# Attention scores from queries and keys in two fp32r parts, and y's remainder written over its source

## The chip, the cores and the metric

The kernel runs on one core of a Trainium2 chip. The metric is the device time of one execution, in microseconds (us). Five engines work side by side: TensorE (PE; its weight loads are listed as PEld), VectorE (DVE), ScalarE (ACT), GpSimd (POOL), and SyncE (SP), which here only issues transfers. Each runs its own list of instructions in order and waits for the others on semaphores.

## The reference

One layer of a vision transformer on 16 images of 256 tokens with 256 features:

```python
h = layernorm(patchify(x) @ W) * gamma
# attention, 16 heads of 64, with a decay in place of a softmax
q, k, v = silu(xn @ Wq), silu(xn @ Wk), xn @ Wv
cum = cumsum(-softplus(xn @ Wa + ba))
attn = (q @ k.T) * exp(cum[i] - cum[j])        # for j <= i
o = groupnorm(attn @ v) * gn_w + gn_b
h = h + (o * sigmoid(xn @ Wg)) @ Wo
# feed-forward: the two best of 8 experts for each token
h = h + sum(weight * (gelu(xf @ w1[e] + b1[e]) @ w2[e] + b2[e]))
```

## The kernel before, in words

The 16 images are taken in eight pairs p (`NPR`), and each pair's 16 heads in eight head pairs c (`NP`): two heads of 64 features fill the 128 partitions. An index u says which image of the pair is meant. After the attention stage comes the expert stage; it is not changed but for the place of two buffers.

All matrix products but a few small ones are of one kind: an operand is split into a high part (a copy that rounds to fp32r, made on ScalarE) and a remainder (source minus high part, made on VectorE), and `three` lists the three products high x high, high x low, low x high. The scores were an exception: plain fp32 products of queries and keys.

Every engine has its own function `step(p, c)`, in which the order of its work is written out by hand; `last_step` is step 7. Step c works on the scores of head pair c and prepares head pair c+1 (in step 7, head pair 0 of the next pair). For attention alone:

- TensorE: `scores(c, 0)`, `queries(c+1)`, `weighted(c, 0)`, `scores(c, 1)`, `keys(c+1)`, `gates(c+1)`, `weighted(c, 1)`. Between them stand parts of other work: `values`, the token projection of the next pair (`tokens`), its transposes (`turn`, L1122), `logits`, `out_proj`, routing.
- ScalarE: `keep_o` (copies the output bank, L822), `tanh_q` (L789), `decay(c+1, 0)` (four exponentials, L817), now and then `keep_v`, `affined`, `y_hi` (L835) or `softplus`, then `tanh_k` (L794), `decay(c+1, 1)`, `tanh_g`.
- VectorE: `decayed(c, 0)` (scores times decay, L1674), `silu_q(c+1)` (L1658), other work, `decayed(c, 1)`, `silu_k(c+1)` (L1665), other work. In step 2 the embedding of an image (`embed`, to L1609) stands behind `silu_k`; in step 3 its norm (`embed_norm`, L1617) does.
- GpSimd: `decay_rows` masks the decay rows of the head pair after (L654); in between it raises variances to a power (`embed_rsqrt`, L660, among others) and scatters rows.

A score call (`scores`, L1187) handles one image and one head pair. It makes for each of the two heads, in rows 0 to 63 and 64 to 127 of the array, a product of 256 columns (L1195) and one of 128 (L1198); the causal half that is not needed is left out. Queries and keys lie in two buffers each (`q_s`, `k_s`), used in turn. One tile, `tq`, takes tanh of the queries and then that of the keys.

y is the gated output of the attention. It is split too: `y_hi` writes `y_sp[0]`, `y_lo` (L1722) writes `y_sp[1]`, from `osb`, and `out_proj` multiplies both with the parts of Wo (L1237).

Of the kernel before, what the change touches and what calls it, by code (L numbers as in the profile page):

```python
# [19 lines left out]
F32 = mybir.dt.float32  # L20
# [7 lines left out]
P = 128  # L28
# [47 lines left out]
def vit_layer(nc, xT, w_tok, gamma, wq, wk, wv, wg, wa, ba, wo, gn_w, gn_b,  # L76
# [3 lines left out]
    with ExitStack() as ctx:  # L80
# [41 lines left out]

        ys = [sb(f"y_sp{j}", [P, 2048], F32R) for j in range(2)]
        y_sp = [y[:, :].rearrange("p (k n) -> p k n", k=GC) for y in ys]

        w1_sp = [parts((0, 2048), 2048, EC), parts((10240, 14336), 2048, EC)]
        w2_sp = [parts((4096, 6144), 2048, HC), [y[:, :].rearrange("p (k n) -> p k n", k=HC) for y in ys]]
# [10 lines left out]

        big_f = sb("big_f", [P, 8192])
        stage_w = [big_f[:, i:i + 2048] for i in (0, 2048, 6144)]  # L140
        tg = big_f[:, 0:4096].rearrange("p (k n) -> p k n", k=NP)
        osb = big_f[:, 4096:8192].rearrange("p (k n) -> p k n", k=NP)
        w1_f = [big_f[:, i * 2048:(i + 1) * 2048] for i in range(2)]
# [10 lines left out]
        q_s = [sb(f"q_s{i}", [P, SP2]) for i in range(2)]  # L154
        k_s = [sb(f"k_s{i}", [P, SP2]) for i in range(2)]
# [55 lines left out]
        gel_u = [x[:, i * BLK:(i + 1) * BLK] for x in q_s + k_s for i in range(2)]  # L211
# [68 lines left out]
        v_ps v_done q_ps k_ps g_ps tq_done tk_done tg_done sq_done sk_done s_ps mult_done o_ps o_done gst_done  # L280
# [66 lines left out]
        def _(sp):  # L347
# [144 lines left out]
            def load_next_early(j):  # L492
# [14 lines left out]
                if j == 1:  # L507
                    sp.wait_ge(M["sk_done"], NP * NPR)
# [237 lines left out]
        def _(act):  # L746
# [39 lines left out]
            def tanh_q(p, c):  # L786
                act.wait_ge(M["q_ps"], NP * p + c + 1)
                have(act, "sk_done", NP * p + c)
# [21 lines left out]
            def decay(p, c, u):  # L810
# [3 lines left out]
                for hh in range(2):  # L814
# [17 lines left out]
            def y_hi(p, g, j):  # L832
                act.wait_ge(M["gate_done"], 4 * p + 2 * g + j + 1)
                have(act, "wo_ps", 2 * (2 * p + g))
                act.activation(y_sp[0][:, 2 * j:2 * j + 2, :], osb[:, GC * g + 2 * j:GC * g + 2 * j + 2, :], ACT.Copy).then_inc(M["yh_done"], 1)  # L835
# [73 lines left out]
            def last_step(p):  # L909
# [17 lines left out]
                if nxt:  # L927
                    tanh_k(p + 1, 0)
                    keep_v(p + 1, 1, 0)
                    decay(p + 1, 0, 1)  # L930
                    tanh_g(p + 1, 0)

            def step(p, c):
# [167 lines left out]
        def _(pe):  # L1101
# [1120 lines left out]
```

## Time and profile before

| | us |
|---|---|
| median of 3 runs (1324.74 to 1326.38) | 1326.38 |
| the profiled execution | 1323.79 |
| its span | 1321.9 |
| TensorE busy | 1250.9 (95%) |
| ScalarE busy | 858.5 (65%) |
| VectorE busy | 825.2 (62%) |
| GpSimd busy | 428.1 (32%) |

The span goes from the first instruction of the program to the last in one profiled execution. The attention stage fills about the first 833 us of it, the expert stage the rest. Busy times are sums over an engine's instructions; TensorE's products overlap, so their single durations add up to more than the time that passes. The granted clock is the share of full speed that TensorE was given. A bracket at the end of a row of the timeline tells how long the engine was idle before it and what ended that.

### The profile page before, as it was taken

The numbers are of one execution on the slowest core, as the hardware profiler recorded it, in microseconds if no ns is written. First come the engines' busy times: TensorE is split into PE (matmuls) and PEld (weight loads), VectorE is DVE, ScalarE is ACT, GpSimd is POOL, SyncE is SP. The second block draws the span as 40 slices with busy tenths as digits, with TensorE's granted clock in tenths as the row PEclk, the third lists the DMA queues.
The fourth block names the chain that finished last, engine by engine and source line by source line (L and its number), as shares of the span: only waits on it lengthen the run. The fifth ranks groups of instructions, "written<-read, shape, count | busy, mean of one in ns | idle before, by whom it ended". The sixth has DMA issues, their size and how long they took to land. (4 is left out here: it accounts for less than half of the span.)

```text
span 1321.9 us, 27298 instructions
## 1 busy us (share of the span) xinstructions
PE 1250.9 (95%) x8534; PEld 1072.3 (81%) x8534; DVE 825.2 (62%) x2119; ACT 858.5 (65%) x2019; POOL 428.1 (32%) x524
## 2 busy tenths in 40 slices
PE   3899999999999999999999999999999999999996
PEld 2676777878778778778778778889999999989996
DVE  4455556665665665665665566657788888565552
ACT  2557577576576576576576565636788888666662
POOL 2021211241241241241141142164444544433434
PEclk7799999999999999999999999999999999999998
DMA  5321331341331331341332236458888787888873
GB/s 193 121 93 61 105 98 47 117 131 46 117 129 49 109 128 57 108 130 57 108 114 63 89 102 186 161 179 245 282 238 222 222 237 188 262 257 262 249 232 88
DMA packets 125607, 194.46 MB, mean 147 GB/s; under 512 B 16272, under 2 KB 91504, under 8 KB 125360
## 3 DMA queue, kind: packets, MB, share of 16 engines
q1 hardware_dynamic: 111920, 175.91, 41.5%
q0 software_dynamic: 13584, 17.26, 6.4%
q8 instruction: 54, 0.88, 0.3%
q14 instruction: 49, 0.40, 0.1%
HBM read 167.40 MB, written 29.05 MB: 149 GB/s over the span
## 5 line engine op out<-in xcount | busy, mean ns | idle before, releaser
L1161 PE MATMUL bank<-xn_sp,big_r 128*128 128x512 f32 x1152 | 312.1, 408 | 0.0
L1161 PEld LDWEIGHTS bank<-xn_sp,big_r 128*128 128x128 f32 x1152 | 204.6, 188 | 53.2 <-issue 1.4
L1674 DVE TENSOR_TENSOR att<-bank,dec_x 128x384 f32<-128x384 f32 x256 | 130.7, 552 | 110.1 <-PE bank L1198 108.9
L817 ACT ACTIVATE dec_x<-dec_x,ncum 128x256 f32<-128x256 f32 (+1 forms) x512 | 189.7, 444 | 5.7 <-POOL dec_x L654 5.7
L654 POOL TENSOR_SCALAR_AFFINE_SELECT dec_x<-dec_x 128x256 f32<-128x256 f32 x256 | 103.6, 434 | 215.8 <-DMA dec_x<-cum_scratch 215.7
L1494 PE MATMUL bank<-big_r 128*128 128x256 f32 x1296 | 168.0, 286 | 1.5 <-ACT mid_f L887 1.0
L1494 PEld LDWEIGHTS bank<-big_r 128*128 128x128 f32 x1296 | 160.5, 192 | 3.3 <-ACT mid_f L887 1.4
L705 POOL TENSOR_SCALAR mid_f<-mid_f,dec_x 128x256 f32<-128x256 f32 x71 | 76.9, 1087 | 187.0 <-DVE mid_f L1925 184.6
L711 POOL DMA_INDIRECT out<-mid_f,tok x71 | 118.6, 1671 | 53.0 <-POOL mid_f L705 22.0
L1941 DVE TENSOR_TENSOR big_r<-mid_f,big_r 128x256 fp32r<-128x256 f32 x216 | 91.4, 424 | 69.5 <-ACT big_r L907 69.3
L887 ACT ACTIVATE mid_f<-bank,h 128x256 f32<-128x256 f32 x216 | 101.2, 477 | 43.5 <-PE bank L1494 22.1
L789 ACT ACTIVATE tq<-bank 128x512 f32<-128x512 f32 x64 | 38.3, 598 | 140.3 <-PE bank L1161 140.3
L1932 DVE TENSOR_TENSOR big_r<-big_f,big_r 128x512 fp32r<-128x512 f32 x148 | 102.0, 695 | 7.1 <-ACT big_r L881 0.4
L1154 PE MATMUL bank<-big_r,xn_sp 128*128 128x512 f32 x384 | 97.7, 393 | 0.0
L1237 PEld LDWEIGHTS bank<-big_r,y_sp 128*128 128x128 f32 x768 | 95.5, 191 | 1.9
L1237 PE MATMUL bank<-big_r,y_sp 128*128 128x256 f32 x768 | 96.8, 284 | 0.0
L794 ACT ACTIVATE tq<-bank 128x512 f32<-128x512 f32 x64 | 38.2, 596 | 89.2 <-PE bank L1161 89.1
L1209 PE MATMUL bank<-att,mid_f 128*64 128x256 f32 x512 | 85.6, 407 | 10.4 <-ACT big_f L822 8.0
L1195 PE MATMUL bank<-q_s,k_s 64*128 64x256 f32 x512 | 91.0, 432 | 4.2 <-issue 4.2
L676 POOL DMA_INDIRECT expert_rows<-xn,slot x64 | 69.0, 1078 | 76.6 <-DVE slot L1809 60.4
L881 ACT ACTIVATE big_r<-big_f 128x512 fp32r<-128x512 f32 x148 | 93.5, 636 | 0.0
L907 ACT ACTIVATE big_r<-mid_f 128x256 fp32r<-128x256 f32 x216 | 91.7, 425 | 0.0
(217 smaller groups left out, 2231.4 us busy)
## 6 DMA issues: line engine op xcount, KB each, us to landing
big_f<-in_L_ffn_w SPq DMA_DIRECT2D x68, 1024.0 KB, 6.2
dec_x<-cum_scratch SPq DMA_DIRECT2D x128, 384.0 KB, 3.5
big_w<-in_L_ffn_w SPq DMA_DIRECT2D x12, 1024.0 KB, 6.7
mid_f<-expert_rows SPq DMA_DIRECT2D x27, 261.0 KB, 3.4
xt<-in_x SPq DMA_DIRECT2D x16, 256.0 KB, 3.7
h_scratch<-h SPq DMA_DIRECT2D x16, 256.0 KB, 2.3
h<-h_scratch SPq DMA_DIRECT2D x8, 512.0 KB, 4.3
out<-h SPq DMA_DIRECT2D x16, 256.0 KB, 4.0
```

Of the source, the lines that this page charges most:

```text
L654: pool.affine_select(out=d, in_=d, pattern=[[0, 2], [1, P]], compare_op=ALU.is_ge, fill=fill, base=0, channel_multiplier=-1).then_inc(M["c ...
L711: pool.indirect_dma_start(out=out_rows, out_offset=bass.IndirectOffsetOnAxis(ap=tok[k.par][:, s:s + 1], axis=0), in_=yo[k.par][:, s, :], i ...
L817: act.activation(d, d, ACT.Exp, bias=ncum[p % 2][:, NS * u + s, 2 * c + hh:2 * c + hh + 1]).then_inc(M["exp_done"], 1)
L881: act.activation(parts[0].rearrange("p k n -> p (k n)")[:, cols], staged[:, cols], ACT.Copy).then_inc(M[f"{name}_hi"], 1)
L887: act.activation(target, bank[hbank[c % HB]][:, 0:width], ACT.Gelu_apprx_tanh, bias=b1_sb[k.par][:, c:c + 1]).then_inc(M["gel_done"], 1)
L907: act.activation(g_sp[0][:, c, :], gel[c % NGEL], ACT.Copy).then_inc(M["gh_done"], 1)
L1154: mm = pe.matmul(bank[target][:, :], xp[:, k, t * P:(t + 1) * P], wp[:, k, n * 512:(n + 1) * 512], start=(k == 0 and j == 0), stop=(k == E ...
L1161: mm = pe.matmul(bank[target][:, :], wp[:, k, c * P:(c + 1) * P], xp[:, k, :], start=(k == 0 and j == 0), stop=(k == EC - 1 and j == 2))
L1237: mm = pe.matmul(bank[target][:, s * E:(s + 1) * E], yp[:, j, u * S + s * P:u * S + (s + 1) * P], wp[:, GC * g + j, :], start=(j == 0 and ...
L1494: mm = pe.matmul(bank[hbank[c % HB]][:, 0:BLK], wp[:, i, c * P:(c + 1) * P], xp[:, i, :], start=(i == 0 and j == 0), stop=(i == EC - 1 and ...
L1674: dve.tensor_tensor(att[hh][:, :], bank[4 + hh][:, 0:LW], dec[n % RING][:, hh, :], ALU.mult).then_inc(M["mult_done"], 1)
L1932: dve.tensor_tensor(lo, staged[:, cols], f32(hi), ALU.subtract).then_inc(M[f"{name}_lo"], 1)
```

## The change

Four things are done:

- The silu of queries stays in `tq`, that of keys goes to a tile of its own, `tk`. Each is then split: `q_hi` and `k_hi` are copies on ScalarE, `q_lo` and `k_lo` subtractions on VectorE. The four parts of queries and keys fill one tile, `qk_sp`, of the size that `q_s` and `k_s` had, so they lie once, not twice.
- `scores` makes the three products of the parts: six products of 256 columns and six of 128 in a call, where it made two and two.
- In `step`, `q_hi` stands ahead of `tanh_k`, `q_lo` behind `decayed(c, 1)`, `k_hi` between the exponentials of the two heads of `decay(c+1, 1)`, and `k_lo` right behind `silu_k`.
- y's remainder is written over its source: `big_lo` names the place of `big_f` as fp32r, and `olo` is its half that holds `osb`. What writes there later (`keep_o`, and two loads of expert weights) now waits for `out_proj`, which reads it, in place of `y_lo`. The high part has `ys[1]`; `ys[0]` is used in the expert stage only.

```diff
-        q_s = [sb(f"q_s{i}", [P, SP2]) for i in range(2)]
-        k_s = [sb(f"k_s{i}", [P, SP2]) for i in range(2)]
+        qk_sp = sb("qk_sp", [P, 4 * SP2], F32R)
+        q_sp = [qk_sp[:, i * SP2:(i + 1) * SP2] for i in range(2)]
+        k_sp = [qk_sp[:, i * SP2:(i + 1) * SP2] for i in range(2, 4)]
...
                 if j == 1:
-                    sp.wait_ge(M["sk_done"], NP * NPR)
+                    sp.wait_ge(M["ql_done"], NP * NPR)
...
                 if isinstance(k.b, int) and k.b < 2:
-                    sp.wait_ge(M["yl_done"], 4 * NPR - 2 + 2 * k.b)
+                    sp.wait_ge(M["wo_ps"], 4 * NPR - 2 + 2 * k.b)
...
             def tanh_k(p, c):
                 act.wait_ge(M["k_ps"], NP * p + c + 1)
-                act.wait_ge(M["sq_done"], NP * p + c + 1)
-                act.activation(tq[:, :], bank[1][:, :], ACT.Tanh, scale=0.5).then_inc(M["tk_done"], 1)
+                have(act, "kl_done", NP * p + c)
+                act.activation(tk[:, :], bank[1][:, :], ACT.Tanh, scale=0.5).then_inc(M["tk_done"], 1)
+
+            def q_hi(p, c):
+                n = NP * p + c
+                act.wait_ge(M["sq_done"], n + 1)
+                have(act, "s_ps", 4 * n)
+                act.activation(q_sp[0], tq[:, :], ACT.Copy).then_inc(M["qh_done"], 1)
+
+            def k_hi(p, c):
+                n = NP * p + c
+                act.wait_ge(M["sk_done"], n + 1)
+                have(act, "s_ps", 4 * n)
+                act.activation(k_sp[0], tk[:, :], ACT.Copy).then_inc(M["kh_done"], 1)
...
             def keep_o(p, c):
                 act.wait_ge(M["o_ps"], 2 * NP * p + 2 * c + 2)
-                have(act, "yl_done", 4 * (p - 1) + c // 2 + 1)
+                have(act, "wo_ps", 4 * (p - 1) + 2 * (c // GC) + 2)
...
                 if main:
+                    q_hi(p, c + 1)
                     tanh_k(p, c + 1)
                 if c == 6 and post:
                     keep_x2(2 * p - 1)
                 if main:
-                    decay(p, c + 1, 1)
+                    decay(p, c + 1, 1, (0,))
+                    k_hi(p, c + 1)
+                    decay(p, c + 1, 1, (1,))
...
             def scores(p, c, u):
                 n = 4 * (NP * p + c) + 2 * u
-                pe.wait_ge(M["sq_done"], NP * p + c + 1)
-                pe.wait_ge(M["sk_done"], NP * p + c + 1)
+                pe.wait_ge(M["ql_done"], NP * p + c + 1)
+                pe.wait_ge(M["kl_done"], NP * p + c + 1)
                 have(pe, "mult_done", n)
...
+                qs, ks = ([x[:, u * S:(u + 1) * S] for x in y] for y in (q_sp, k_sp))
+                for j, (k, q) in enumerate(three(ks, qs)):
+                    for hh in range(2):
+                        r = slice(D * hh, D * hh + D)
+                        pe.matmul(bank[4 + hh][:, 0:S], k[r, 0:P], q[r, :], start=(j == 0), stop=(j == 2))
+                for j, (k, q) in enumerate(three(ks, qs)):
+                    for hh in range(2):
+                        r = slice(D * hh, D * hh + D)
+                        mm = pe.matmul(bank[4 + hh][:, S:LW], k[r, P:S], q[r, P:S], start=(j == 0), stop=(j == 2))
+                        if j == 2:
+                            mm.then_inc(M["s_ps"], 1)
...
+            def k_lo(p, c):
+                n = NP * p + c
+                dve.wait_ge(M["kh_done"], n + 1)
+                dve.tensor_tensor(k_sp[1], tk[:, :], f32(k_sp[0]), ALU.subtract).then_inc(M["kl_done"], 1)
...
             def y_lo(p, g, j):
                 cs = slice(GC * g + 2 * j, GC * g + 2 * j + 2)
                 dve.wait_ge(M["yh_done"], 4 * p + 2 * g + j + 1)
-                dve.tensor_tensor(y_sp[1][:, 2 * j:2 * j + 2, :], osb[:, cs, :], f32(y_sp[0][:, 2 * j:2 * j + 2, :]), ALU.subtract).then_inc(M["yl_done"], 1)
+                dve.tensor_tensor(olo[:, cs, :], osb[:, cs, :], f32(y_hi_sp[:, 2 * j:2 * j + 2, :]), ALU.subtract).then_inc(M["yl_done"], 1)
...
                 if main:
                     decayed(p, c, 1)
+                    q_lo(p, c + 1)
                 if c == 4 and post:
                     residual(2 * p - 2)
                 if main:
                     silu_k(p, c + 1)
+                    k_lo(p, c + 1)
```

## Rows read from the trace of the kernel before

**Rows 1.** The page, busy time and instructions of each engine.
```profile
PE 1250.9 (95%) x8534; PEld 1072.3 (81%) x8534; DVE 825.2 (62%) x2119; ACT 858.5 (65%) x2019; POOL 428.1 (32%) x524
```

**Rows 2.** One pair: busy time and count of each engine, granted clock, DMA share, GB/s.
```profile
347.00:447.30 100.30, 98.59 (x641) 78.77 (x641) 63.26 (x166) 64.87 (x147) 28.78 (x46) 1.00 0.29 97
```

**Rows 3.** Timeline, TensorE, one score call: start, time taken (us), engine, line, operation, count.
```profile
407.80 0.70 PE L1195 MATMUL bank<-q_s,k_s 64*128 64x256 f32 x4
408.34 0.39 PE L1198 MATMUL bank<-q_s,k_s 64*128 64x128 f32 x4
408.65 0.50 PE L1161 MATMUL bank<-xn_sp,big_r 128*128 128x512 f32 x1
```

**Rows 4.** Timeline, weight loads of that call: the first pair, and both pairs.
```profile
407.80 0.19 PEld L1195 LDWEIGHTS bank<-q_s,k_s 64*128 64x128 f32 x2 [0.17 <-issue]
...
407.80 0.30 PEld L1195 LDWEIGHTS bank<-q_s,k_s 64*128 64x128 f32 x4 [0.17 <-issue]
```

**Rows 5.** Groups by line and shape: count | busy us, mean ns | idle us before.
```profile
L1195 PE MATMUL bank<-q_s,k_s 64*128 64x256 f32 x512 | 91.0, 432 | 4.2 <-issue 4.2
L1198 PE MATMUL bank<-q_s,k_s 64*128 64x128 f32 x512 | 50.2, 272 | 0.0
...
L881 ACT ACTIVATE big_r<-big_f 128x512 fp32r<-128x512 f32 x148 | 93.5, 636 | 0.0
...
L1932 DVE TENSOR_TENSOR big_r<-big_f,big_r 128x512 fp32r<-128x512 f32 x148 | 102.0, 695 | 7.1 <-ACT big_r L881 0.4
```

**Rows 6.** Timeline, TensorE, and the same instructions' group: the output projection.
```profile
394.74 3.03 PE L1237 MATMUL bank<-big_r,y_sp 128*128 128x256 f32 x24
...
L1237 PE MATMUL bank<-big_r,y_sp 128*128 128x256 f32 x768 | 96.8, 284 | 0.0
```

**Rows 7.** Timeline, step 0 of pair 3: the key chain and the scores after it.
```profile
355.50 0.60 ACT L794 ACTIVATE tq<-bank 128x512 f32<-128x512 f32 x1 [2.76 <-PE bank L1161]
356.13 0.69 DVE L1665 SCALAR_TENSOR_TENSOR k_s<-tq,bank 128x512 f32<-128x512 f32 x1 [0.43 <-ACT tq L794]
...
357.81 0.70 PE L1195 MATMUL bank<-q_s,k_s 64*128 64x256 f32 x4
```

**Rows 8.** Timeline, step 5 of pair 3: the key chain behind softplus.
```profile
414.33 1.28 ACT L794 ACT_TABLE_LOAD   x1
...
416.26 0.69 DVE L1665 SCALAR_TENSOR_TENSOR k_s<-tq,bank 128x512 f32<-128x512 f32 x1 [2.31 <-ACT tq L794]
...
417.05 0.70 PE L1195 MATMUL bank<-q_s,k_s 64*128 64x256 f32 x4 [0.53 <-issue]
```

**Rows 9.** Timeline, step 3 of pair 3: from the power to the transposes.
```profile
383.43 1.04 POOL L660 TENSOR_TENSOR rs<-rs,mhalf 128x4 f32<-128x4 f32 x1 [1.86 <-DVE rs L1609]
...
385.25 1.49 ACT L817 ACTIVATE dec_x<-dec_x,ncum 128x256 f32<-128x256 f32 x4 [0.37 <-POOL dec_x L654]
...
387.12 1.05 ACT L835 ACTIVATE y_sp<-big_f 128x1024 fp32r<-128x1024 f32 x1
388.92 0.60 ACT L794 ACTIVATE tq<-bank 128x512 f32<-128x512 f32 x1 [0.75 <-PE bank L1161]
...
389.55 0.69 DVE L1665 SCALAR_TENSOR_TENSOR k_s<-tq,bank 128x512 f32<-128x512 f32 x1 [1.11 <-ACT tq L794]
390.15 0.73 DVE L1617 TENSOR_SCALAR turned<-h,st1u,rs 128x256 f32<-128x256 f32 x2
...
391.03 0.63 PE L1122 MATMUL bank<-ident,turned 128*128 128x128 f32 x4 [0.76 <-DVE turned L1617]
```

**Rows 10.** Timeline, steps 6 and 7 of pair 3: tanh, and the wait for the output bank.
```profile
424.19 0.60 ACT L794 ACTIVATE tq<-bank 128x512 f32<-128x512 f32 x1 [0.65 <-PE bank L1161]
...
431.74 0.65 PE L1209 MATMUL bank<-att,mid_f 128*64 128x256 f32 x4 [0.42 <-ACT big_f L822]
```

**Rows 11.** Lines L1122 and L1209: what ended TensorE's idle time before them, us, times.
```profile
  DVE turned L1617: 19.3, 9
...
  ACT big_f L822: 18.8, 16
```

More of the change, by code:

```diff
@@ L121, in parts @@
             return [big_r[:, f:f + size].rearrange("p (k n) -> p k n", k=chunks) for f in first]
+        with nc.sbuf_tensor("tk", [P, SP2], F32) as tk:
+            pass
         ys = [sb(f"y_sp{j}", [P, 2048], F32R) for j in range(2)]
-        y_sp = [y[:, :].rearrange("p (k n) -> p k n", k=GC) for y in ys]
         w1_sp = [parts((0, 2048), 2048, EC), parts((10240, 14336), 2048, EC)]
-        w2_sp = [parts((4096, 6144), 2048, HC), [y[:, :].rearrange("p (k n) -> p k n", k=HC) for y in ys]]
+        w2_sp = [parts((4096, 6144), 2048, HC), [y[:, :].rearrange("p (k n) -> p k n", k=HC) for y in (ys[1], ys[0])]]
         g_sp = parts((8192, 12288), HC * BLK, HC)
@@ L136, in vit_layer @@
         wt = sb("wt", [P, KT + 1, E])
+        with nc.sbuf_tensor("big_lo", [P, 8192], F32R) as big_lo:
+            pass
         big_f = sb("big_f", [P, 8192])
@@ L210, in vit_layer @@
         w1_stage = [w1_f[0], w1_x]
-        gel_u = [x[:, i * BLK:(i + 1) * BLK] for x in q_s + k_s for i in range(2)]
+        gel_u = [gel_w[:, i * BLK:(i + 1) * BLK] for i in range(HC)]
         gel_1 = [gel_u[c // 2][:, (c % 2) * P:(c % 2 + 1) * P] for c in range(HC)]
@@ L787, in tanh_q @@
                 act.wait_ge(M["q_ps"], NP * p + c + 1)
-                have(act, "sk_done", NP * p + c)
+                have(act, "ql_done", NP * p + c)
                 act.activation(tq[:, :], bank[0][:, :], ACT.Tanh, scale=0.5).then_inc(M["tq_done"], 1)
@@ L808, in keep_v, with decay @@
                 act.activation(v_sb[:, t, n * 512:(n + 1) * 512], bank[source][:, :], ACT.Copy).then_inc(M["v_done"], 1)
-            def decay(p, c, u):
+            def decay(p, c, u, heads=(0, 1)):
                 n = 2 * NP * p + 2 * c + u
@@ L813, in decay @@
                 act.wait_ge(M["ncum_done"], p + 1)
-                for hh in range(2):
+                for hh in heads:
                     for s, cols in ((0, slice(0, S)), (1, slice(S, LW))):
@@ L1234, in out_proj @@
                     for s in range(NS):
-                        for q, (wp, yp) in enumerate(three(wo_sp, y_sp)):
+                        for q, (wp, yp) in enumerate(three(wo_sp, (y_hi_sp, olo[:, GC * g:GC * g + GC, :]))):
                             mm = pe.matmul(bank[target][:, s * E:(s + 1) * E], yp[:, j, u * S + s * P:u * S + (s + 1) * P], wp[:, GC * g + j, :],
@@ L1656, in silu_q, with q_lo @@
                 dve.wait_ge(M["tq_done"], n + 1)
-                have(dve, "s_ps", 4 * (n - 1))
-                dve.scalar_tensor_tensor(out=q_s[c % 2][:, :], in0=tq[:, :], scalar=1.0, in1=bank[0][:, :],
+                dve.scalar_tensor_tensor(out=tq[:, :], in0=tq[:, :], scalar=1.0, in1=bank[0][:, :],
                                          op0=ALU.add, op1=ALU.mult).then_inc(M["sq_done"], 1)
+            def q_lo(p, c):
+                n = NP * p + c
+                dve.wait_ge(M["qh_done"], n + 1)
+                dve.tensor_tensor(q_sp[1], tq[:, :], f32(q_sp[0]), ALU.subtract).then_inc(M["ql_done"], 1)
             def silu_k(p, c):
@@ L1663, in silu_k @@
                 dve.wait_ge(M["tk_done"], n + 1)
-                have(dve, "s_ps", 4 * (n - 1))
-                dve.scalar_tensor_tensor(out=k_s[c % 2][:, :], in0=tq[:, :], scalar=1.0, in1=bank[1][:, :],
+                dve.scalar_tensor_tensor(out=tk[:, :], in0=tk[:, :], scalar=1.0, in1=bank[1][:, :],
                                          op0=ALU.add, op1=ALU.mult).then_inc(M["sk_done"], 1)
+            def k_lo(p, c):
+                n = NP * p + c
+                dve.wait_ge(M["kh_done"], n + 1)
+                dve.tensor_tensor(k_sp[1], tk[:, :], f32(k_sp[0]), ALU.subtract).then_inc(M["kl_done"], 1)
             def decayed(p, c, u):
```

22 lines of the change are left out of this document (12 added, 10 removed).

## The prediction

> **What bounds the kernel now.** I read the page first: the profiled execution took 1323.79 us, its span is 1321.9 us, and TensorE is busy for 95% of it [rows 1]. Then I cut out one period of the attention stage, pair 3, from the first score product of its head pair 0 to that of pair 4. It lasts 100.3 us: TensorE is busy for 98.6 of them at a granted clock of 1.00, ScalarE for 65 and VectorE for 63 [rows 2]. So TensorE sets the pace, and the other two have a third of their time free. What the change costs is therefore decided at the few places where TensorE already waits, or nearly waits, for one of them. I looked for those places in the timeline, head pair by head pair, and found four that matter [rows 7 to 10]. "Step c" is below the stretch that starts with the first score call of head pair c and prepares the queries and keys of c+1.
>
> **The change on TensorE.** A score call was two fp32 products of 256 columns and two of 128, one per head, on the upper and lower 64 rows of the array. The trace shows each as two instructions. Four of the wide ones take 0.70 us in all [rows 3] though one lasts 432 ns [rows 5], so the two heads overlap; the call runs from 407.80 to the next projection at 408.65, that is 0.85 us [rows 3]. Its parts: the first weight load shows for 0.11 us (two pairs of loads take 0.30 us where one pair takes 0.19 [rows 4]), the last product starts at 408.46 (408.34 + 0.39 - 0.27 [rows 3, 5]), and 0.19 us later the projection begins.
>
> After the change a call has six pairs of fp32r products, each one instruction with its own weights: three pairs of 256 columns, three of 128. No row has fp32r on half the rows, nor on 128 columns. Lower bound per pair: 0.11 us, the distance of weight loads on half the rows [rows 4]. Upper bound for the wide ones and, I think, the narrow ones too: 0.12 us, the pace of full-array fp32r products of 256 columns (24 in 3.03 us, the last of them 0.28 [rows 6]). I take 0.12, because it is fp32r, as they are: 0.11 + 5 x 0.12 + 0.19 = 0.90 us, 0.05 more than now; with 0.11, and a last product of half the length, 0.80. So three products cost about what the fp32 form costs: +0.05 x 128 calls = +7 us, with -6 us as the other end. The Trainium skill ("TensorE: Matmul & The Clock Gate", Back-to-back issue gap) gives 81 ns for a sustained pair of load and matmul of 128 columns. The trace does not agree for 4-byte operands: its paces are 0.11 and 0.12 us. By that figure of the Trainium skill a call would take 0.11 + 5 x 0.08 + 0.19 = 0.70 us, an estimate; what that would make of the time is rival (e).
>
> **The copies.** Each of the 64 steps gets two high parts on ScalarE and two remainders on VectorE, all 128x512. The nearest rows are the copies of the expert weights: 0.64 us and 0.70 us [rows 5]. That is 82 and 89 us of work that fits into the free third; as bare load I cost it at nothing, with the idle time of rows 2 as its cover. What counts is where it sits in the chains. A handoff costs 0.03 us (355.50 + 0.60 to 356.13 [rows 7]); an engine begins its next instruction some 0.09 us before the last one ends (389.55 + 0.69 against 390.15 [rows 9]), so a copy holds ScalarE for 0.54 and VectorE for 0.61 us.
>
> The key chain was keys, tanh, silu, scores. It becomes keys, tanh, silu, high part (ScalarE, behind the first head's two exponentials, which end before silu does), remainder, scores: longer by 0.03 + 0.64 + 0.03 + 0.70 = 1.40 us. Queued behind the remainder's wait on VectorE is everything that step does after silu of k, also later by 1.40. The query chain is ready long before the keys, so its copies matter only as load in front of tanh and silu of k.
>
> Step 0: silu of k ends at 356.82 (356.13 + 0.69), the remainder at 358.22, scores 0.07 later at 358.29; they start at 357.81 now [rows 7]. Cost 0.5 us.
>
> Step 5: softplus stands before tanh of k. A table load of 1.28 us follows its Ln at 414.33 [rows 8]. The query's high part goes in front of that load and moves the chain behind it by 0.64: silu of k, now 416.26 to 416.95, ends at 417.59, the remainder at 418.99, scores start at 419.06 instead of 417.05 [rows 8]. TensorE waits there already (0.53 us), so all 2.0 us land.
>
> Steps 2 and 3: a longer chain. The embedding of the next pair stands behind silu of k in step 2 and moves by 1.40. GpSimd's power (383.43) waits for that embedding, the causal masks for head pair 4 stand behind the power on GpSimd, and ScalarE's exponentials wait for these masks now (0.37 us before 385.25) [rows 9]. They start at 386.65. Behind them on ScalarE: the y high part, which ended at 388.17 and ends at 389.57, then the new query copy (0.54), then tanh of k at 390.02 instead of 388.92. VectorE's query remainder holds it to 390.77, where silu of k starts, instead of 389.55. Silu ends at 391.46, the remainder at 392.86, and the norm of the next image, now at 390.15, begins at 392.77: 2.6 us later. TensorE's transposes of that norm wait for it now (0.76 us [rows 9]), so all 2.6 land, and it is no odd event: waits of this kind add up to 19.3 us over nine places [rows 11], and they stand ahead of the weighted sums of step 3 and everything behind. The 0.2 us by which the weighted sums of step 3 come later lie within it.
>
> Step 7: TensorE waits for ScalarE's copy of the output bank (0.42 us before 431.74 [rows 10]); such waits come 16 times, 18.8 us in all [rows 11]. From tanh of k in step 6 to that copy ScalarE works without a gap, so the key's high part, 0.54 us, lands: 0.5 us. The query's is hidden in the 0.65 us that ScalarE waits for the keys before that tanh [rows 10].
>
> Elsewhere the longer key chain is covered by what TensorE does between keys and scores (values, output projection, token projection); if that cover were gone, each of the other six first score calls of a pair could cost up to 1.4 us.
>
> The rest has one answer: y's remainder is written in place, no instruction more. Its reader, the output projection, is ahead of the next output copy in TensorE's own order, so the new wait of that copy costs nothing. SP's waits for the projection and for the query remainder stand behind later waits of SP, or are met earlier. The double buffer of q and k is gone, but the new high parts follow the last score call of the step before in any case.
>
> **Sum.** 0.5 + 2.6 + 2.0 + 0.5 = 5.6 us per pair. Pairs 0 to 6 have all four: 39 us. Pair 7 has neither softplus nor an embedding behind it: I count the 0.5 and about 1.4 for the table work behind its first key remainder, 2 us. Score calls: +7; four of them per pair stand ahead of waits that shrink as they grow, -1. Together +47 us on 1323.8: 1371 us. The median of the runs, 1326.38, is 2.6 above the profiled one.
>
> **Rivals.** (a) A narrow fp32r product costs what an fp32 one of its shape costs, 0.21 us (four of 128 columns in 0.39 us, the last of them 0.27: two pairs 0.11 apart [rows 3, 5]). Against it: the full-array rows show fp32r at one instruction. A call takes 0.11 + 3 x 0.12 + 2 x 0.21 + 0.11 + 0.19 = 1.19, that is +0.34 x 128 = +44, of which 8 hide in the waits: 1323.8 + 41 + 44 - 8 = 1401 us. (b) fp32r products on the two halves do not overlap: 0.11 + 11 x 0.12 + 0.19 = 1.62 a call, +99, 14 hidden: 1450 us. Against it: fp32 ones do [rows 3]. (c) The chain through GpSimd has slack that I don't see, and only the waits at steps 0, 5 and 7 land: 7 x 3.0 + 2 + 6 = 29, 1353 us. (d) The other side: the loads of half-array fp32r weights hide behind the products, so that a call takes three times 0.107 and three times 0.053 us of streaming (256 and 128 columns at the 2.4 GHz that rows 2 grant) with little around it. It gets even where a call is down by 41 / 128 = 0.32, to 0.53 us. Against it: rows 4, where loads stand 0.11 apart. Then 1324 us. (e) Weight loads of half the rows come faster than rows 4 show, so that the pairs follow each other in 0.08 us instead of 0.12 and a call takes 0.70: -0.15 x 128 = -19 us, 4 of which go to waits that then show, 1323.8 + 41 - 19 + 4 = 1350 us. That is the pace that the Trainium skill gives (the same section of "TensorE: Matmul & The Clock Gate"); rows 4 and 6 speak against it.
>
> **How the numbers follow.** Forecast 0.57, (a) 0.20, (b) 0.05, (c) 0.10, (d) 0.03, (e) 0.05. The range takes in (c), (e) and the lower end of the score calls below, and (a) above: 1345 to 1410; outside are (b), (d) and edges. A measurement of this kernel tells about 0.2% from no change. All cases but (d) are slower by more; (d) is split between the other two.
>
> **What would show it.** A score call near 0.90 us from its first load to the next projection; six pairs at 0.12. Scores of head pair 1 waiting some 0.5 us and of head pair 6 some 2.5 us (0.53 now). The transposes in step 3 waiting some 3.4 us for VectorE. A period of 100.3 + 5.6 + 0.8 = 106.7 us less 0.2. The expert stage as long as before. A call of 1.2 us speaks for (a), of 1.6 for (b). What I would have wrong first: the chain of step 3, which goes through three engines, and TensorE's clock, if waits of 3 us make its grant fall below 1.00.

## The result

The changed kernel takes 1403.61 us (median of 4 runs, 1398.43 to 1404.72), the kernel before 1325.56 us (4 runs, 1324.70 to 1326.38). The ratio is 1.0581, with an interval of 1.0553 to 1.0609: it is slower by 78 us. The profiled execution took 1403.16 us, its span is 1401.3 us, and TensorE's mean granted clock over the span is 0.953 (0.983 before). The time lies inside the range of 1345 to 1410, but 33 us above the forecast of 1371.

The page of the changed kernel, busy time and instructions of each engine (against [rows 1]):

```profile
PE 1288.0 (92%) x9046; PEld 1112.2 (79%) x9046; DVE 911.5 (65%) x2247; ACT 931.7 (66%) x2147; POOL 445.8 (32%) x524
```

512 products more (four in each of 128 score calls), and 128 instructions more on VectorE and on ScalarE, as planned. These two did not become the bound: each is busy for about two thirds of the span, as before.

The windows of the changed kernel: pair 3 cut as before, pair 2, and the attention stage; columns as in [rows 2] (busy time and count of PE, PEld, DVE, ACT, POOL, granted clock, DMA share, GB/s):

```profile
380.30:487.80 107.50, 100.09 (x704) 81.37 (x703) 73.96 (x182) 73.83 (x163) 31.39 (x46) 0.98 0.28 91
265.60:380.30 114.70, 107.30 (x706) 86.77 (x705) 73.91 (x182) 74.00 (x163) 31.95 (x46) 0.91 0.27 85
...
50.00:905.00 855.00, 792.54 (x5390) 637.56 (x5388) 560.26 (x1321) 573.31 (x1261) 221.45 (x347) 0.95 0.28 91
```

And most of the attention stage of the kernel before:

```profile
50.00:830.00 780.00, 760.04 (x4875) 601.60 (x4875) 474.46 (x1194) 500.94 (x1134) 204.61 (x347) 1.00 0.31 100
```

Two things are to be seen. In pair 3 TensorE is idle for 7.4 us (107.50 less 100.09) where it was idle for 1.7. And the clock, 1.00 in [rows 2], is 0.98 in pair 3 and 0.91 in pair 2, though both hold the same work. Pair 2 lasts 7.2 us longer than pair 3, and all of that is busy time (107.30 against 100.09). The last weighted sum of the stage starts at 833.0 us before and at 909.9 us after: 76.9 us of the loss lie in the attention stage.

The four places of [rows 7 to 10] in the timeline of the changed kernel, TensorE, pair 3: a score call and its follower, then the first scores of head pair 1, the transposes of step 3, the scores of head pair 6, and the weighted sum of step 7 (start, time taken, engine, line, operation, count, idle time before and what ended it):

```profile
391.80 0.62 PE L1222 MATMUL bank<-qk_sp 64*128 64x256 f32 x6 [0.54 <-issue]
...
420.47 0.62 PE L1222 MATMUL bank<-qk_sp 64*128 64x256 f32 x6
420.93 0.45 PE L1226 MATMUL bank<-qk_sp 64*128 64x128 f32 x6
421.31 0.50 PE L1187 MATMUL bank<-xn_sp,big_r 128*128 128x512 f32 x1
...
427.79 0.63 PE L1148 MATMUL bank<-ident,turned 128*128 128x128 f32 x4 [3.44 <-DVE turned L1647]
...
457.17 0.61 PE L1222 MATMUL bank<-qk_sp 64*128 64x256 f32 x6 [2.47 <-issue]
...
472.35 0.65 PE L1239 MATMUL bank<-att,mid_f 128*64 128x256 f32 x4 [0.96 <-ACT big_f L842]
```

The waits are 0.54, 3.44, 2.47 and 0.96 us; before, they were 0, 0.76, 0.53 and 0.42 [rows 7 to 10]. The score call is no dearer: from 420.47 to the next projection at 421.31 it takes 0.84 us, against 0.85 in [rows 3]. Over the whole trace, what TensorE's products waited for (us in total, times, longest), in the changed kernel and then in the kernel before:

```profile
PE bank L1148 <- DVE turned L1647: 36.1, 9, 6.8
PE bank L1222 <- issue: 25.1, 19, 2.9
PE bank L1239 <- ACT big_f L842: 11.9, 8, 3.8
...
PE bank L1122 <- DVE turned L1617: 19.3, 9, 7.2
PE bank L1209 <- ACT big_f L822: 8.0, 8, 3.2
...
PE bank L1195 <- issue: 4.2, 7, 1.0
```

The output copy stands in [rows 11] with 18.8 us and 16 times because that view lists the products and, once more, their weight loads; the products alone waited 8 times. Of the nine waits at the transposes two, of 6.7 to 7.2 us, fall into the first 33 us of the execution, in both kernels. The other seven, one in each of pairs 0 to 6, sum to 5.4 us before and to 22.6 after.

The chain of step 3 in the changed kernel, from the power to the norm (timeline of pair 3; for the transposes that wait for the norm, see 427.79 above):

```profile
418.74 1.04 POOL L668 TENSOR_TENSOR rs<-rs,mhalf 128x4 f32<-128x4 f32 x1 [3.64 <-DVE rs L1639]
...
420.56 1.49 ACT L837 ACTIVATE dec_x<-dec_x,ncum 128x256 f32<-128x256 f32 x4 [1.82 <-POOL dec_x L662]
422.44 1.05 ACT L855 ACTIVATE y_sp<-big_f 128x1024 fp32r<-128x1024 f32 x1
423.39 0.62 ACT L808 ACTIVATE qk_sp<-tq 128x512 fp32r<-128x512 f32 x1
423.91 0.58 ACT L802 ACTIVATE tk<-bank 128x512 f32<-128x512 f32 x1
...
424.64 0.68 DVE L1698 SCALAR_TENSOR_TENSOR tk<-tk,bank 128x512 f32<-128x512 f32 x1
426.02 0.69 DVE L1704 TENSOR_TENSOR qk_sp<-tk,qk_sp 128x512 fp32r<-128x512 f32 x1 [0.69 <-ACT qk_sp L814]
426.63 1.01 DVE L1647 TENSOR_SCALAR turned<-h,st1u,rs 128x256 f32<-128x256 f32 x2
```

Against [rows 9]: ScalarE waits 1.82 us for the masks (0.37 before), which stand behind the power on GpSimd; the query's high part (L808) stands between y and tanh, and the norm (L1647) now stands behind the key's remainder, which itself waited 0.69 us for the high part.

What the forecast had not priced is seen right behind these waits. The score call that follows the transposes, 1.8 us after the wait's end (timeline of the changed kernel, TensorE, pair 3):

```profile
429.63 1.01 PE L1222 MATMUL bank<-qk_sp 64*128 64x256 f32 x6
430.44 0.73 PE L1226 MATMUL bank<-qk_sp 64*128 64x128 f32 x6
431.10 0.80 PE L1187 MATMUL bank<-xn_sp,big_r 128*128 128x512 f32 x1
```

Windows of the changed kernel: around that call, and the 13.5 us from the scores of head pair 6 on, in pair 2 and in pair 3:

```profile
428.70:431.90 3.20, 3.20 (x22) 2.48 (x19) 0.96 (x3) 1.51 (x3) 1.35 (x3) 0.50 0.24 87
343.30:356.80 13.50, 13.09 (x60) 10.86 (x61) 6.47 (x18) 6.78 (x15) 3.10 (x5) 0.50 0.01 1
457.20:470.70 13.50, 13.50 (x105) 11.66 (x106) 10.32 (x23) 12.18 (x27) 3.10 (x5) 1.00 0.02 5
```

The call at 429.63 takes 1.47 us in place of 0.84, at a clock of 0.50, the lower of the two levels. In pair 2 the stretch behind the wait of head pair 6 (2.46 us there) runs at 0.50 throughout, and 60 products are done in the time in which pair 3, at 1.00, does 105. Added up from the trace's record of the grant, TensorE is at half clock (a grant of 0.50) for 85.3 us of the attention stage, counted from 50 us on to the last weighted sum, against 6.8 us before.

### The profile page after: what moved, and what is told of

It is laid out like the page before. It is cut to its first block and busy times, and to the rows that moved or that the text cites. A ratio compares the mean times of both kernels' runs of the same rounds, so it can differ in the third digit from the quotient of the medians.

```text
span 1401.3 us, 28643 instructions
## 1 busy us (share of the span) xinstructions
PE 1288.0 (92%) x9046; PEld 1112.2 (79%) x9046; DVE 911.5 (65%) x2247; ACT 931.7 (66%) x2147; POOL 445.8 (32%) x524
## 5 line engine op out<-in xcount | busy, mean ns | idle before, releaser
L1187 PE MATMUL bank<-xn_sp,big_r 128*128 128x512 f32 x1152 | 324.3, 420 | 0.0
L1187 PEld LDWEIGHTS bank<-xn_sp,big_r 128*128 128x128 f32 x1152 | 213.3, 196 | 49.7 <-issue 1.2
L837 ACT ACTIVATE dec_x<-dec_x,ncum 128x256 f32<-128x256 f32 (+1 forms) x512 | 195.8, 443 | 20.6 <-POOL dec_x L662 20.6
L662 POOL TENSOR_SCALAR_AFFINE_SELECT dec_x<-dec_x 128x256 f32<-128x256 f32 x256 | 123.8, 515 | 229.2 <-DMA dec_x<-cum_scratch 229.1
L797 ACT ACTIVATE tq<-bank 128x512 f32<-128x512 f32 x64 | 38.3, 598 | 140.0 <-PE bank L1187 140.0
L1222 PE MATMUL bank<-qk_sp 64*128 64x256 f32 x768 | 84.6, 327 | 26.8 <-issue 25.1
L1239 PE MATMUL bank<-att,mid_f 128*64 128x256 f32 x512 | 92.1, 425 | 13.5 <-ACT big_f L842 11.9
L1222 PEld LDWEIGHTS bank<-qk_sp 64*128 64x128 f32 x768 | 57.6, 197 | 51.2 <-issue 50.3
L673 POOL TENSOR_TENSOR gr<-gr,mhalf 128x8 f32<-128x8 f32 x16 | 26.2, 1639 | 216.3 <-DVE gr L1737 216.3
L684 POOL DMA_INDIRECT expert_rows<-xn,slot x64 | 65.4, 1022 | 71.2 <-DVE slot L1847 55.1
```

The costliest lines, as they stand in the source:

```text
L662: pool.affine_select(out=d, in_=d, pattern=[[0, 2], [1, P]], compare_op=ALU.is_ge, fill=fill, base=0, channel_multiplier=-1).then_inc(M["c ...
L837: act.activation(d, d, ACT.Exp, bias=ncum[p % 2][:, NS * u + s, 2 * c + hh:2 * c + hh + 1]).then_inc(M["exp_done"], 1)
L1187: mm = pe.matmul(bank[target][:, :], wp[:, k, c * P:(c + 1) * P], xp[:, k, :], start=(k == 0 and j == 0), stop=(k == EC - 1 and j == 2))
L1222: pe.matmul(bank[4 + hh][:, 0:S], k[r, 0:P], q[r, :], start=(j == 0), stop=(j == 2))
```

## The experiments

Each is named with the kernel it was made from. All ratios are to the kernel before, measured on the same chip beside it.

**The three products without the copies** (from the kernel before; the lines of buffers left out).

```diff
-        q_s = [sb(f"q_s{i}", [P, SP2]) for i in range(2)]
-        k_s = [sb(f"k_s{i}", [P, SP2]) for i in range(2)]
+        qk_sp = sb("qk_sp", [P, 4 * SP2], F32R)
+        q_s = [qk_sp[:, i * SP2:(i + 1) * SP2] for i in range(2)]
+        k_s = [qk_sp[:, i * SP2:(i + 1) * SP2] for i in range(2, 4)]
...
-                for hh in range(2):
-                    r = slice(D * hh, D * hh + D)
-                    pe.matmul(bank[4 + hh][:, 0:S], k[r, 0:P], q[r, :], start=True, stop=True)
+                for j in range(3):
+                    for hh in range(2):
+                        r = slice(D * hh, D * hh + D)
+                        pe.matmul(bank[4 + hh][:, 0:S], k[r, 0:P], q[r, :], start=(j == 0), stop=(j == 2))
```

> The kernel before, with the score calls alone changed: silu writes queries and keys once, rounded to fp32r, and a call makes six pairs of fp32r products, all of these same parts. No copies and no remainders are made, so the output lacks the remainders' share and the product is added three times. Theory (the products cost nothing, the time goes to waits and to the clock that falls after them): a call takes 0.84 us as in the changed kernel, 0.01 less than before, 128 calls make -2 us, time 1322 to 1327 us. Rival (the three products cost time of their own, which the waits only hide): over 1335 us, with calls of 0.9 us or more.

Measured: 1325.48 us (1322.41 to 1327.41, 10 runs), ratio 1.000 (0.9987 to 1.0013). A score call in its timeline:

```profile
407.25 0.62 PE L1199 MATMUL bank<-qk_sp 64*128 64x256 f32 x6
407.71 0.45 PE L1203 MATMUL bank<-qk_sp 64*128 64x128 f32 x6
408.08 0.50 PE L1164 MATMUL bank<-xn_sp,big_r 128*128 128x512 f32 x1
```

Its window of pair 3:

```profile
346.50:446.80 100.30, 98.46 (x707) 80.17 (x707) 63.29 (x167) 64.87 (x147) 28.50 (x46) 1.00 0.29 98
```

The call takes 0.83 us and the pair 100.30 us, to the tenth what it takes in [rows 2]. Twelve fp32r products cost what four fp32 ones did. The rivals (a) and (b), by which the products carry the loss, and (d) and (e), by which they give much back, fall here.

**y in place alone** (from the kernel before).

```diff
-                have(act, "yl_done", 4 * (p - 1) + c // 2 + 1)
+                have(act, "wo_ps", 4 * (p - 1) + 2 * (c // GC) + 2)
...
-                dve.tensor_tensor(y_sp[1][:, 2 * j:2 * j + 2, :], osb[:, cs, :], f32(y_sp[0][:, 2 * j:2 * j + 2, :]), ALU.subtract).then_inc(M["yl_done"], 1)
+                dve.tensor_tensor(olo[:, cs, :], osb[:, cs, :], f32(y_hi_sp[:, 2 * j:2 * j + 2, :]), ALU.subtract).then_inc(M["yl_done"], 1)
```

> The kernel before with the second part of the change alone: y's remainder is written over its source, the output copy and two weight loads wait for the output projection. Theory: no instruction more, and every wait is met before it is asked, 1324 to 1328 us. Rival: the output copy of a later step or the weight loads now wait for the projection, over 1330 us.

Measured: 1325.91 us (1323.28 to 1328.14), ratio 1.0009 (0.9996 to 1.0022). The part costs nothing that can be measured. With the products free as well, what is left to carry the loss is the copies, in their place in the chains, and the buffers of queries and keys, which lie once.

**Products that nobody reads, in the two long waits** (from the changed kernel). They do not shorten a wait; they only keep TensorE at work in it.

```diff
             def turn(n):
                 pe.wait_ge(M["s1_u"], NS * (n + 1))
+                if n % 2 and n >= 3:
+                    for i in range(12):
+                        pe.matmul(bank[6][:, :], wsp[0][0][:, 0, 0:P], xn_sp[0][:, 0, :], start=True, stop=True)
                 pe.wait_ge(M["s1_xn"], NS * (n + 1))
...
+                have(pe, "mult_done", n)
+                if c == 6 and u == 0 and p < NPR - 1:
+                    for i in range(9):
+                        pe.matmul(bank[4][:, :], wsp[0][0][:, 0, 0:P], xn_sp[0][:, 0, :], start=True, stop=True)
                 pe.wait_ge(M["ql_done"], NP * p + c + 1)
                 pe.wait_ge(M["kl_done"], NP * p + c + 1)
-                have(pe, "mult_done", n)
```

> The changed kernel, with products that nobody reads put into TensorE's two longest waits of each pair: 12 of 512 columns ahead of the transposes of step 3 (wait 3.44 us), 9 ahead of the scores of head pair 6 (wait 2.47 us). The waits stay as long as they are, only TensorE is not idle in them. Theory (some 30 of the 78 us are half clock after these waits): the stretches of half clock in the attention stage, some 85 us in all in the changed kernel, go below 25 us, every pair takes 106 to 108 us as pair 3 does, time 1365 to 1382 us. Rival (the waits alone cost all of it, the clock falls anyway or costs nothing): 1398 to 1410 us.

Measured: 1370.66 us (1368.07 to 1374.70), ratio 1.0338 (1.0306 to 1.0370). Its timeline at the two waits of pair 3:

```profile
412.81 2.88 PE L1147 MATMUL bank<-xn_sp,big_r 128*128 128x512 f32 x12
416.32 0.66 PE L1151 MATMUL bank<-ident,turned 128*128 128x128 f32 x4 [0.63 <-issue]
...
441.70 2.34 PE L1221 MATMUL bank<-xn_sp,big_r 128*128 128x512 f32 x9
444.29 0.62 PE L1228 MATMUL bank<-qk_sp 64*128 64x256 f32 x6 [0.25 <-DVE qk_sp L1710]
```

Its window of pair 2:

```profile
262.80:368.90 106.10, 103.63 (x727) 84.11 (x726) 73.82 (x182) 73.88 (x163) 31.17 (x46) 1.00 0.29 92
```

The waits for useful work are as long as in the changed kernel (412.81 to 416.32, 3.51 us; 441.70 to 444.29, 2.59 us), but pair 2 now lasts 106.1 us at a clock of 1.00, where it lasted 114.7 at 0.91. So the clock takes 1403.6 - 1370.7 = 33 us of the loss, and the rest, the waits above all, 1370.7 - 1325.2 (the kernel before in that comparison) = 45 us. Half clock remains for 17.1 us of the attention stage; (85.3 - 17.1) / 2 = 34 us is about the same amount from the other side, if half clock costs half the stretch.

**Keys not split** (from the changed kernel): it tells what the key's two copies are worth.

```diff
-                    k_hi(p, c + 1)
...
-                dve.scalar_tensor_tensor(out=tk[:, :], in0=tk[:, :], scalar=1.0, in1=bank[1][:, :],
+                have(dve, "s_ps", 4 * n)
+                dve.scalar_tensor_tensor(out=k_sp[0], in0=tk[:, :], scalar=1.0, in1=bank[1][:, :],
                                          op0=ALU.add, op1=ALU.mult).then_inc(M["sk_done"], 1)
...
-                    k_lo(p, c + 1)
```

> The changed kernel without the split of the keys: silu writes the keys' high part at once, there is no high copy and no remainder of keys, and the third product takes the high part again, so the output lacks the share of the keys' remainder. Queries are split as in the change, TensorE has the same products. Theory (the key chain, 1.40 us longer, makes the waits): the wait of the scores of head pair 1 goes, that of head pair 6 is 1.1 us (0.53 and the query copy's 0.64), the transposes of step 3 wait 1.3 to 1.6 us, half clock is nearly gone, time 1328 to 1342 us. Rival (load of ScalarE and VectorE as such, of which half stays): some 1360 us or more.

Measured: 1328.54 us (1326.34 to 1332.59), ratio 1.0024 (1.0009 to 1.0040). Timeline of pair 3, scores of head pair 1, transposes, scores of head pair 6:

```profile
359.73 0.62 PE L1220 MATMUL bank<-qk_sp 64*128 64x256 f32 x6
...
392.81 0.63 PE L1146 MATMUL bank<-ident,turned 128*128 128x128 f32 x4 [0.86 <-DVE turned L1645]
...
419.30 0.62 PE L1220 MATMUL bank<-qk_sp 64*128 64x256 f32 x6 [1.08 <-issue]
```

Without the key's high part and remainder nearly all of the loss is gone: 75 of 78 us. At head pair 6 half a microsecond more than before stays, which is the query's copy ahead of the table load. The transposes wait 0.86 us, hardly more than the 0.76 of [rows 9], where 1.3 to 1.6 had been expected: the query's two copies are nearly hidden in that chain. The buffers that lie once are in this kernel too, so they cost next to nothing.

**The norm ahead of the key's silu in step 3** (from the changed kernel).

```diff
                     decayed(p, c, 1)
+                if c == 3 and nxt:
+                    embed_norm(2 * p + 3)
+                if main:
                     q_lo(p, c + 1)
...
                 if c == 3:
-                    if nxt:
-                        embed_norm(2 * p + 3)
```

> The changed kernel, with the norm of the next image in step 3 moved on VectorE from behind the keys' remainder to a place ahead of the query remainder, where VectorE is idle for 1.14 us. Nothing is left out. Theory (the transposes' wait of 3.44 us is that norm standing behind the key chain): the wait goes, but the scores of head pair 4 then meet the key chain itself (its remainder ends at 426.71 in the changed kernel, and they would start some 1.1 us before) and wait about 1.1 us; no half clock after step 3 any more, that after the scores of head pair 6 stays: 2.3 us for each of seven pairs and some 8 us of clock, time 1370 to 1388 us. Rival (the 3.44 us are not from this order but from the chain through GpSimd): the wait of 3 us shows in full at the scores of head pair 4, time over 1395 us.

Measured: 1368.93 us (1367.06 to 1370.70), ratio 1.0319 (1.0301 to 1.0337), slightly less than the expected 1370 to 1388. Timeline of pair 3, the norm on VectorE and the scores of head pair 4 on TensorE:

```profile
410.87 0.72 DVE L1647 TENSOR_SCALAR turned<-h,st1u,rs 128x256 f32<-128x256 f32 x2
...
414.87 0.63 PE L1222 MATMUL bank<-qk_sp 64*128 64x256 f32 x6 [1.23 <-issue]
```

The transposes no longer wait, and the scores of head pair 4, next in line for the same VectorE, wait 1.23 us instead: 2.2 of the 3.4 us are won. 47.8 us of half clock remain of 85.3: that is worth some 19 us, where 8 had been expected. A norm that was queued behind a remainder it has nothing to do with cost, with its part of the clock, 35 us.

**The query's copies late in steps 3 and 5** (from the changed kernel).

```diff
-                    q_hi(p, c + 1)
+                    if c not in (3, 5):
+                        q_hi(p, c + 1)
                     tanh_k(p, c + 1)
...
+                if main and c in (3, 5):
+                    q_hi(p, c + 1)
+                    k_hi(p, c + 1)
+                    decay(p, c + 1, 1)
...
                     silu_k(p, c + 1)
+                    if c in (3, 5):
+                        q_lo(p, c + 1)
                     k_lo(p, c + 1)
```

> The changed kernel, with the query's high part in steps 3 and 5 behind tanh of the keys on ScalarE, the keys' high part right after it, both ahead of the exponentials, and the query's remainder behind silu of the keys on VectorE. Nothing is left out. Theory: the key chain keeps its 1.40 us, but the query copies no longer stand ahead of it: the scores of head pair 6 wait 1.8 instead of 2.47 us, the transposes of step 3 2.8 instead of 3.44: 1.25 us for each of seven pairs, and up to 15 us of clock: 1380 to 1396 us. Rival (the query copies are hidden where they stand): 1398 us or more.

Measured: 1387.52 us (1382.61 to 1387.87), ratio 1.0447 (1.0425 to 1.0468). Its waits:

```profile
PE bank L1154 <- DVE turned L1653: 28.0, 8, 6.7
...
PE bank L1228 <- DVE qk_sp L1699: 14.1, 7, 2.4
...
PE bank L1154 <- issue: 2.6, 1, 2.6
```

The transposes' nine waits fall from 36.1 us to 28.0 + 2.6 = 30.6 (the profile names no engine for one of them). Those of head pair 6, 2.47 us in pair 3 of the changed kernel, fall to 1.94 there (14.1 us over pairs 0 to 6), where 1.8 had been expected. The query's high part no longer stands ahead of the table load, but it and its remainder (L1699) now stand between tanh of k and the key's remainder, which gives a part of it back. In this order or the other, the query's copies are the smaller part of the loss.

**All orders together** (from the changed kernel): the two edits above, and

```diff
-                    y_hi(p, 0, 0)
                     keep_o(p, 6)
+                    y_hi(p, 0, 0)
...
-                    k_lo(p, c + 1)
+                    if c != 2:
+                        k_lo(p, c + 1)
...
                 if c == 2:
                     if post:
                         gated(p - 1, 1, 1)
+                    if main:
+                        k_lo(p, c + 1)
                     if nxt:
                         embed(2 * p + 3)
```

> The changed kernel with four moves and nothing left out: the two before, the keys' remainder of step 2 behind the gating, and in step 7 the copy of the output bank ahead of y's high part on ScalarE. Theory: no wait at the transposes, little at the scores of head pair 4, 1.8 us at those of head pair 6, 0.5 at head pair 1, none at the output copy, clock as in the kernel before: 1323.8 + 7 x (0.5 + 1.3 - 0.6 - 0.4) + 2 + 3 to 10 for what is late next, 1332 to 1345 us, still above the kernel before, since the products gain nothing. Rival (the copies as load on ScalarE and VectorE cost time wherever they stand): 1355 us or more.

Measured: 1352.46 us (1344.81 to 1356.77), ratio 1.0189 (1.0156 to 1.0222): above the expected 1332 to 1345. The scores of head pair 6 of pair 3 in its timeline:

```profile
433.65 0.62 PE L1228 MATMUL bank<-qk_sp 64*128 64x256 f32 x6 [1.95 <-DVE qk_sp L1699]
```

Its windows behind that wait, in pair 3 and in pair 4:

```profile
433.50:443.00 9.50, 9.35 (x53) 7.87 (x54) 5.35 (x18) 6.73 (x16) 3.10 (x5) 0.61 0.01 2
539.20:549.00 9.80, 9.67 (x75) 8.50 (x75) 6.85 (x20) 9.15 (x21) 3.10 (x5) 1.00 0.01 3
```

One wait of 1.95 us stays (the profile names the query's remainder; the key's, L1710, is the last to end, at 433.55), and behind it the clock is 0.61 in pair 3 and 1.00 in pair 4. Was the miss the clock? That was tried next.

**All orders, and unread products in the wait that is left** (from the kernel just shown).

```diff
+                have(pe, "mult_done", n)
+                if c == 6 and u == 0 and p < NPR - 1:
+                    for i in range(7):
+                        pe.matmul(bank[4][:, :], wsp[0][0][:, 0, 0:P], xn_sp[0][:, 0, :], start=True, stop=True)
                 pe.wait_ge(M["ql_done"], NP * p + c + 1)
                 pe.wait_ge(M["kl_done"], NP * p + c + 1)
-                have(pe, "mult_done", n)
```

> The kernel with four moves, and seven products of 512 columns that nobody reads ahead of the scores of head pair 6 in pairs 0 to 6, where TensorE waits 2.16 us. Theory (what is left over the forecast of 1332 to 1345 us is half clock after that wait, 47.6 us of it in the attention stage, 13.6 of them in the last two pairs, whatever is done): the stretches in pairs 0 to 5 go and give some 34 / 2 = 17 us, less what of them falls into waits anyway: time 1333 to 1342 us. Rival (the copies as load cost the rest): 1348 us or more.

Measured: 1338.72 us (1333.44 to 1341.49), ratio 1.0087 (1.0062 to 1.0112). It was the clock: 14 us; half clock in the attention stage falls from 47.8 us to 10.2. This is the fastest version tried with the full split of queries and keys; 65 of the 78 us are undone, by order and by unread products, with no copy taken away. What the other 13 us are was not taken apart.

**The same orders in the kernel before**, without the change: norm ahead of `silu_k` in step 3, `keep_o` ahead of `y_hi` in step 7.

```diff
-                    y_hi(p, 0, 0)
                     keep_o(p, 6)
+                    y_hi(p, 0, 0)
...
                     decayed(p, c, 1)
+                if c == 3 and nxt:
+                    embed_norm(2 * p + 3)
```

> The kernel before, without the change, with two of these moves: the norm of the next image ahead of silu of the keys in step 3, the copy of the output bank ahead of y's high part in step 7. Nothing is left out. Theory: the waits of 0.62 and 0.42 us of each pair go, 7 x 0.62 + 8 x 0.42 = 7.7 us if nothing else is late there: 1317 to 1321 us, less than both kernels. Rival (the work behind them, tanh of the keys or y's high part, becomes the wait): 1323 to 1327 us.

Measured: 1314.71 us (1311.13 to 1317.72), ratio 0.9903 (0.9887 to 0.9920): faster than both kernels, 1% faster than the kernel before, and 2 us below the expected range. The transposes and the weighted sum of step 7 in its timeline, pair 3:

```profile
386.87 0.60 PE L1122 MATMUL bank<-ident,turned 128*128 128x128 f32 x4
...
427.09 0.65 PE L1209 MATMUL bank<-att,mid_f 128*64 128x256 f32 x4
```

Its window of pair 3:

```profile
343.60:442.60 99.00, 98.46 (x640) 78.92 (x639) 63.34 (x166) 64.65 (x147) 28.46 (x46) 1.00 0.29 99
```

The two waits of [rows 9, 10] are gone (no bracket), and the pair lasts 99.0 us instead of 100.3: of the 1.3 us, 0.76 and 0.42 are those of the rows. The same two places that the change makes worse were open before it.

## Why the prediction held, and where it fell short

**The sign, and the mechanism.** Right as far as the waits go. They sit at the four places that were named, where TensorE waits for chains that go through ScalarE, VectorE and GpSimd. The other part of the loss, the clock, has a paragraph below.

**Step 0.** Forecast 0.5 us, measured 0.54.

**Step 5.** The wait was forecast to grow from 0.53 to 2.5 us; it is 2.47. The query's copy stands ahead of the table load as was read from [rows 8].

**Steps 2 and 3.** Forecast 3.4 us, measured 3.44, and link by link. Counted from the start of the pair (347.00 before, 380.30 after) and less the 0.54 us of step 0, the exponentials start 420.56 - 380.30 - 0.54 - (385.25 - 347.00) = 1.47 us later, where 1.40 was forecast; tanh of k 1.15 (1.10) and the norm 2.64 (2.6), by the same working from the rows above and [rows 9].

**Step 7.** Forecast 0.42 + 0.5, measured 0.96.

**The sum of the waits.** Forecast 5.6 us a pair and 41 in all. In pair 3 the waits grew by 0.54 + 2.68 + 1.94 + 0.54 = 5.7 us, that is 40 over seven pairs. The run with unread products puts all that is not the filled clock at 45 us. In its profiled execution the attention stage is 883.0 - 833.0 = 50 us longer than before: 3.4 ahead of the first pair, where its first scores wait 1.50 us for the first key remainder and where the forecast had nothing; 42.4 in pairs 0 to 6; 4.2 in pair 7, forecast as 2. The half clock that was left, 17.1 - 6.8 = 10 us, is worth some 5 of the 50.

**The score calls.** The term of +7 us was mis-sized: I took the full-array pace of 0.12 us [rows 6] for all six pairs. The pace lies between the two bounds: six weight loads, three pairs, take 0.41 us in all where two take 0.19 [rows 4], that is 0.11 us a pair. The rest of the call is shorter than I had added it up, too. A call takes 0.84 us, -0.01 x 128 = -1 us. The Trainium skill ("TensorE: Matmul & The Clock Gate", Back-to-back issue gap) gives 81 ns for a load and a product of 128 columns. The paces of 0.11 and 0.12 us that I held against it do not compare with it: 0.11 is that of two loads side by side, one for each half, and 0.12 that of products of 256 columns. What the trace shows is that rival (e), which took the 81 ns for a pair of heads, is wrong: a call of twelve takes 0.84 us and not 0.70.

**The clock.** This is the step that failed: the sum was made throughout at the 1.00 of [rows 2]. The prediction named the fall of the grant behind waits of 3 us as what could be wrong first, but put no price on it, though the waits that it forecast were of that very size. It was worth 33 us, nearly half of the loss and as much as the gap between 1371 and 1403.6 (32.6 us). That the rest, 45 us, comes so near the forecast's 47 is in part luck: the +7 of the score calls did not come, and 3.4 us ahead of the first pair and some 5 us of half clock that even the unread products left did. The 1.00 of [rows 2] is that of a pair whose longest wait in [rows 7 to 10] is 0.76 us; it tells nothing of waits of 3 us. No row on record ahead of the prediction told of such a wait, but the trace of the kernel before did: in pair 6 TensorE waits 3.21 us for the output copy, and right after it the grant is 0.50 (timeline and window of the kernel before):

```profile
732.83 0.75 PE L1209 MATMUL bank<-att,mid_f 128*64 128x256 f32 x4 [3.21 <-ACT big_f L822]
...
733.30:736.60 3.30, 3.30 (x17) 2.33 (x14) 2.44 (x4) 0.42 (x1) 0.66 (x2) 0.50 0.93 284
```

The score call in that stretch takes 1.59 us (733.93 to 735.52), against 0.85. So a case "every long wait also costs the clock" belonged among the rivals, and it could have been priced from this place.

Of the 33 us some 4 lie in the expert stage, which was forecast as unchanged: behind the last weighted sum come 491.4 us in the changed kernel (1401.3 - 909.9) and 487.5 (1370.5 - 883.0) with unread products, 488.9 before. In the kernel before with two moves, without the change, it is 492.0 (1315.8 - 823.8), so a difference of this size is no sign of the change.

**The rivals.** The time came out at that of rival (a), 1401 us, and for another reason, which was luck: (a) wanted a score call of 1.19 us, and it is 0.84 at full clock. That 1.47 us stand where the clock is at half shows how easily (a) could be taken as shown by looking at one call only. (c) is refuted: the chain through GpSimd has no slack. The range reached to 1410 because of (a), so it held the time for a reason that was not the true one.

**The period.** Forecast 106.5 us. Pair 2 at full clock lasts 106.1 us (the run with unread products). In the changed kernel pairs 1 to 6 last 108.3, 114.7, 107.5, 108.8, 114.8 and 109.3 us: the two long ones are those where the wait of head pair 6 also lost the clock.

**Two readings of [rows 11].** The 16 waits for the output copy are eight, and 14 of the 19.3 us at the transposes lie ahead of pair 0, so "waits of this kind" are seven of some 0.76 us. Neither number entered the sum.

**What stays open.** The grant fell in or right behind each of the waits of 3.2 to 3.5 us in step 3, in pairs 1 to 6. With those of 2.5 us at head pair 6 it fell in pairs 2 and 5 of the changed kernel, and in pairs 1, 2, 4 and 5 of the kernel with the norm ahead; with those of 1.95 us in the reordered kernel it fell in pairs 1 to 6 but for pair 4. What decides between waits of the same length was not tried.

## What to carry to other kernels

A step that is added to a chain between engines costs its whole latency wherever the last engine already waits for that chain, and a part of it where that engine nearly waits; and everything that is queued in order behind the new step's own wait moves with it. So put ahead of it what others wait for (here the norm, and the copy of the output bank): all orders together took back 51 of the 78 us with nothing left out, and two of them make the unchanged kernel faster too. When a forecast says that TensorE will wait for two or three microseconds at a time, price the loss of its clock behind the wait as well: here it cost 33 us beside 45 us of the rest, the waits above all, and products that nobody reads won it back.

## What the runs showed of the hardware

- In a stage in which TensorE was busy for 93% of the time (792.5 of 855 us), its grant, 1.00 before, was 0.50 in the work right behind a wait of 3.44 us (pair 3, 428.70 to 431.90). Behind one of 2.46 us in pair 2 it stayed at 0.50 for 13.5 us of work, behind one of 2.47 us in pair 3 it did not fall at all.
- Unread products in the two longest waits of each pair kept the grant at 1.00 (pair 2: 106.1 us at 1.00, where it had lasted 114.7 us at 0.91).
- Three fp32r products of a high part and a remainder cost no more than one fp32 product of the same shape on half of the array's rows: a call of twelve takes 0.83 to 0.84 us, one of four 0.85.
- fp32r products on the two halves overlap as fp32 ones do: six of 256 columns take 0.62 us in all, where 24 on the full array take 3.03 [rows 6], so that six would take 5 x 0.12 + 0.28 = 0.88.
- A Copy on ScalarE between two functions with different tables (Ln before, tanh behind) brought no table load of its own: the query's copy starts right behind the Ln (452.27), and the one load of 1.28 us comes after it, ahead of tanh (timeline of the changed kernel, ScalarE, step 5 of pair 3):

```profile
452.43 0.61 ACT L808 ACTIVATE qk_sp<-tq 128x512 fp32r<-128x512 f32 x1
453.07 1.28 ACT L802 ACT_TABLE_LOAD   x1
454.36 0.60 ACT L802 ACTIVATE tk<-bank 128x512 f32<-128x512 f32 x1
```
